# Layer-norm statistics of two token blocks in one VectorE instruction that reads them interleaved

## The chip, the cores and the metric

The kernel runs on one core of one Trainium2 chip. The metric is the device time of one execution in microseconds (us), lower is better. In what follows PE is TensorE (its matmuls; PEld its weight loads), DVE is VectorE, ACT is ScalarE, POOL is GpSimd and SP is SyncE.

## What is computed

The input x has 4096 tokens of 256 channels. It is layer-normalised; the normalised rows xn feed two branches whose results are added to x: a Hyena-like block (normalise again, project to 768 columns, two causal convolutions of 128 taps over time with gates between, an output projection) and a gated feed-forward network with integer weights.

```python
def _layernorm(x, axis=-1, eps=1e-05):
    m = jnp.mean(x, axis=axis, keepdims=True)
    v = jnp.var(x, axis=axis, keepdims=True)
    return (x - m) / jnp.sqrt(v + eps)
...
        xn = _layernorm(x, gamma, beta)
        proj = (xn @ W_in + b_in).reshape(Bn, Tn, ORDER + 1, Dn)
        v = proj[:, :, 0, :]
        y = jnp.transpose(v, (0, 2, 1))
        for i, kern in enumerate((k0, k1)):
            xi = jnp.transpose(proj[:, :, i + 1, :], (0, 2, 1))
            y = _fft_conv(y, kern, Tn) * xi
        y = jnp.transpose(y, (0, 2, 1))
        y = y @ W_out + b_out
        return residual + y
...
        gate = jnp.einsum('bsd,hd->bsh', x, wg)
        up = jnp.einsum('bsd,hd->bsh', x, wu)
        h = jax.nn.silu(gate) * up
        return jnp.einsum('bsh,dh->bsd', h, wd)
...
    x = L0_attn_x
    xn = _layernorm(x, axis=-1)
    x = x + _L0_attn_ref(xn, ...) + _L0_ffn_ref(xn, ...)
```

What the change touches is only the mean m and the variance v of each of the 4096 rows of x.

## The kernel before

The 4096 tokens are 32 blocks of 128. A block has its tokens on the 128 partitions, and block b is `res[:, b, :]`, 256 f32 side by side in SBUF; block b + 1 lies 1024 bytes further on. SP loads x in five batches (blocks 0 to 3, 4 to 7, 8 to 15, 16 to 23, 24 to 31; the borders are `CUTS`).

The program has a first stage (to about 70 us), a main stage of 16 groups G (convolutions, with the feed-forward steps beside them) and a last stage that projects out. The change lies in the first stage. There every engine runs through steps b = 1, 2, ... 43, written out by hand, and semaphores tie the engines together:

- DVE, step b: subtracts the rounded half of block b - 1 (`split_x`, L887, tile xT), may normalise a block two ahead (L879, tile ybuf), aggregates the statistics taken one step earlier (`aggregate`, L872, tile mv), may reverse a block (L901, tile xr), evicts projections (L895, L908), takes new statistics (`block_stats`, L866, tile stats), and does its share of the weight preparation (L946 the low half of the projection weights, L1047 the maxima of the taps, L940 the maxima of the integer weights).
- POOL, for each batch: `first_scales` (L1255 to L1258, tile lns: mean and variance become a factor and an offset) once `stats_ready` has counted that batch; `second_scales` (L1264 to L1267); its own normalised blocks (L1272); the weight load issues (L1331 to L1334); and L1327, the other low half of the projection weights.
- ACT normalises (L681), rounds (L685) and reverses (L692) blocks.
- PE, step b: transposes block b once it is normalised (L345), projects blocks that are a few steps back (L320, banks bank_p and bank_c), and transposes integer weights (L394).

The statistics instruction (`bn_stats`, in the profile BATCH_NORM_STATS2) takes 256 elements of a row and gives six numbers: count, mean and sum of squared deviations of the elements at even places, and the same of those at odd places. The aggregation (`bn_aggr`, in the profile BATCH_NORM_AGGREGATE) makes one mean and one variance out of the six. How many blocks get their statistics in which step is the table `STATS`; blocks 0 to 7 get theirs before step 1, ahead of `column_scales` (L924 to L932), which makes the projection weights. The `stats` tile has room for eight blocks and is used in turn.

```python
    STATS = {1: 4, 2: 1, 3: 1, 4: 2, 5: 2, 6: 1, 7: 2, 8: 4, 9: 1, 11: 1, 12: 1, 13: 1, 16: 3}
...
                    ins = nc.vector.bn_stats(stats[:, b % 8, :], res[:, b, :])
...
                    ins = nc.vector.bn_aggr(mv[:, b, :], stats[:, b % 8, :])
```

Of the kernel before, what the change touches and what calls it, by code (L numbers as in the profile page):

```python
# [6 lines left out]
P = 128  # L7
ALU = mybir.AluOpType
# [9 lines left out]
def hyena_ffn_kernel(nc, x, W_in, b_in, k0, k1, gamma, beta, W_out, b_out, w_gate, w_up, w_down, out):  # L18
# [8 lines left out]
    T, D = x.shape[1], x.shape[2]  # L27
    K = k0.shape[2]
    H = w_gate.shape[0]
    NB = T // P  # L30
# [7 lines left out]
    CUTS = (0, 4, 8, 16, 24, NB)  # L38
# [7 lines left out]

    STATS = {1: 4, 2: 1, 3: 1, 4: 2, 5: 2, 6: 1, 7: 2, 8: 4, 9: 1, 11: 1, 12: 1, 13: 1, 16: 3}
    WHI, WLO, PLO, SDG, KMAX = 3, 4, 5, 4, 5
# [36 lines left out]
    EPS = 1e-5  # L85
# [14 lines left out]
    with ExitStack() as ctx:  # L100
        def sb(name, shape, dt=F32):
            return ctx.enter_context(nc.sbuf_tensor(name, shape, dt))

        def sem(name):
            return ctx.enter_context(nc.semaphore(name))
# [5 lines left out]
        res = sb("res", [P, NB, D])  # L111
# [15 lines left out]
        ident32 = sb("ident32", [P, P])  # L127
        stats = sb("stats", [P, 8, 6])
        mv = sb("mv", [P, NB, 2])
        lns = sb("lns", [P, 8, NB])  # L130
# [14 lines left out]
        r1, r2, r1p, nmr, ls0, r2r = (lns[:, i, :] for i in range(6))  # L145
# [8 lines left out]
        def borrow(name, flat, n):  # L154
# [40 lines left out]
        x_loaded = [sem(f"x_loaded{i}") for i in range(NBATCH)]  # L195
# [10 lines left out]
        sdg_mm, sdg_ready = sem("sdg_mm"), sem("sdg_ready")  # L206
        half_stats, stats_ready, r_ready, r2_ready, r2r_ready = (
            sem("half_stats"), sem("stats_ready"), sem("r_ready"), sem("r2_ready"), sem("r2r_ready"))
        xn_ready, x_tp, xh_ready, xl_ready, xra_ready, xrv_ready = (
# [50 lines left out]
        def batch_of(b):  # L260
            return max(m for m in range(NBATCH) if CUTS[m] <= b)
# [584 lines left out]
        def _(dve):  # L846
# [14 lines left out]

            def block_stats(first, last):
                for b in range(first, last):
                    if b in CUTS:
                        dve.wait_ge(x_loaded[batch_of(b)], 16)
                    ins = nc.vector.bn_stats(stats[:, b % 8, :], res[:, b, :])  # L866
                ins.then_inc(half_stats, 1)

            def aggregate(first, last, batches):
                dve.wait_ge(half_stats, batches)  # L870
                for b in range(first, last):
                    ins = nc.vector.bn_aggr(mv[:, b, :], stats[:, b % 8, :])  # L872
                    if b + 1 in CUTS:
                        ins.then_inc(stats_ready, 1)

# [105 lines left out]
            def prepare(slot):  # L981
# [15 lines left out]
                for q in range(PAIRS):  # L997
                    if PAIR_V[q] == slot:
# [8 lines left out]
                                           op0=ALU.mult, op1=ALU.add).then_inc(gnorm_ready, 1)  # L1007
            block_stats(0, 4)
            aggregate(0, 4, 1)
            block_stats(4, 8)  # L1010
            aggregate(4, 8, 2)
            column_scales()

            done = [8]
            for b in range(1, LAST):
                if b - 1 < NB:
                    split_x(b - 1)
                if b + 2 < NB and NORM[b + 2] == "V":
                    normalise(b + 2)
                if b - 1 in STATS and 1 < b <= max(STATS):  # L1020
                    n = STATS[b - 1]
                    aggregate(done[0] - n, done[0], 2 + sum(1 for t in STATS if t < b))
                for p in range(NB):
# [5 lines left out]
                for n in range(NPB):  # L1029
                    if V_AT[PB * n + PB - 1] + 1 == b:  # L1030
                        scale_bank(n)
                if b in STATS:
                    block_stats(done[0], done[0] + STATS[b])
                    done[0] += STATS[b]
                if b == max(STATS):

                    aggregate(NB - STATS[b], NB, 2 + len(STATS))
                if b == WLO:
# [87 lines left out]
            for G in range(NG):  # L1126
                n = SG * G - LATE
# [101 lines left out]
        def _(pool):  # L1229
            chain = [0]  # L1230

            def link(ins):

                chain[0] += 1
                ins.then_inc(pool_chain, 1)
                pool.wait_ge(pool_chain, chain[0])
# [13 lines left out]
            def first_scales(m):  # L1250
                pool.wait_ge(stats_ready, m + 1)
                s = slice(CUTS[m], CUTS[m + 1])
                mean, var = mv[:, s, 0], mv[:, s, 1]
                half_power = minus_half[:, 0:s.stop - s.start]
                link(nc.gpsimd.tensor_scalar(ls0[:, s], var, EPS, None, ALU.add))  # L1255
                link(nc.gpsimd.tensor_tensor(r1[:, s], ls0[:, s], half_power, ALU.pow))
                link(nc.gpsimd.tensor_tensor(nmr[:, s], mean, r1[:, s], ALU.mult))
                nc.gpsimd.tensor_scalar(nmr[:, s], nmr[:, s], -1.0, None, ALU.mult).then_inc(r_ready, 1)  # L1258

            def second_scales(m):  # L1260
                s = slice(CUTS[m], CUTS[m + 1])
                var = mv[:, s, 1]
                half_power = minus_half[:, 0:s.stop - s.start]
                link(nc.gpsimd.tensor_tensor(ls0[:, s], var, r1[:, s], ALU.mult))  # L1264
                link(nc.gpsimd.tensor_tensor(ls0[:, s], ls0[:, s], r1[:, s], ALU.mult))
                link(nc.gpsimd.tensor_scalar(ls0[:, s], ls0[:, s], EPS, None, ALU.add))
                nc.gpsimd.tensor_tensor(r2[:, s], ls0[:, s], half_power, ALU.pow).then_inc(r2_ready, 1)  # L1267
# [154 lines left out]
```

## Time and profile before

| | |
|---|---|
| median of 3 runs | 333.57 us (333.04 to 333.96) |
| profiled execution, its own time | 333.88 us |
| profiled execution, span of the core | 332.0 us |
| granted TensorE clock, mean | 0.997 of full speed |
| PE busy | 303.2 us, 91% of the span |
| DVE busy | 264.5 us, 80% |
| POOL busy | 212.5 us, 64% |
| ACT busy | 179.3 us, 54% |
| first stage | about 0 to 70 us |

Busy time is added up per engine. On DVE the records of neighbouring instructions overlap by some 0.08 us: the next one starts while the last is still in the pipeline. What an instruction costs its engine is therefore the time from its start to the start of the next one, called its slot below, and not its duration. In rows of the timeline the columns are the start, the time, the engine, the line, the operation, what is written and read, and how many instructions were merged into the row; a bracket tells how long the engine had been idle before it and what ended that.

### The profile page before, as it was taken

To read this page: it belongs to the slowest core of one execution; us is meant where nothing else is said; L and a number is where in the kernel's file an instruction comes from. 1 tells how busy PE (TensorE), PEld (TensorE's weight loads), DVE (VectorE), ACT (ScalarE), POOL (GpSimd) and SP (SyncE) were. 2 spreads that over 40 slices of the span, in tenths; PEclk is the share of its full clock that TensorE was granted. 3 is DMA by queue.
4 is the path that set the end of the run, shared out by engine and by line. 5 is a ranking of instruction groups with operands and counts; after the bars stand their busy time and mean duration, and the time that the engine had idled before them with its cause. 6 is when DMAs were issued, how large, how long until landed. Compare 5 with 4: busy or idle time off the path is not lost.

```text
span 332.0 us, 11912 instructions
## 1 busy us (share of the span) xinstructions
PE 303.2 (91%) x4945; PEld 237.7 (72%) x4945; DVE 264.5 (80%) x534; ACT 179.3 (54%) x385; POOL 212.5 (64%) x290
## 2 busy tenths in 40 slices
PE   0379989999999999999999999999999999989993
PEld 0168777887778768777787777778777866658982
DVE  2798999976976888595887879779687777879994
ACT  3676588654544344443545444444445353479991
POOL 3699979377887877788777768868878563200000
PEclk9999999999999999999999999999999999999998
DMA  7994006827987869677786867879688788001345
GB/s 233 350 350 81 2 9 218 347 71 305 387 297 259 337 241 388 201 328 287 282 360 232 360 239 297 323 258 377 218 333 304 279 360 324 8 1 66 126 155 167
DMA packets 22033, 81.01 MB, mean 244 GB/s; under 512 B 1494, under 2 KB 13402, under 8 KB 13786
## 3 DMA queue, kind: packets, MB, share of 16 engines
q1 hardware_dynamic: 19458, 77.47, 62.6%
q0 software_dynamic: 2368, 2.36, 3.7%
q8 instruction: 41, 0.67, 0.8%
q10 hardware_dynamic: 152, 0.40, 0.4%
q14 instruction: 14, 0.11, 0.1%
HBM read 75.50 MB, written 4.72 MB: 242 GB/s over the span
## 4 chain that ended last, share of the span: by engine, by line
PE 49%; DVE 20%; POOL 11%; ACT 8%; issue 7%; DMA 3%; SPq 0%; POOLq 0%; DVEq 0%
PE bank_c L320 13%; PE bank_p L320 11%; PE bank_g L320 9%; PE bank_u L320 9%; PE bank_d L320 7%; ACT vx L834 3%; ACT vx L826 3%; DVE sgh L1055 3%; DMA res<-in_L_attn_x 3%; DVE hhl L1060 2%; DVE vx L908 2%; POOL ybuf L1374 2%; DVE xT L887 2%; POOL vhl L1288 2%; DVE stats L866 1%
## 5 line engine op out<-in xcount | busy, mean ns | idle before, releaser
L320 PE MATMUL bank_d<-wd,hhl 128*128 128x256 f16 x384 | 84.3, 271 | 0.3 <-DVE hhl L1060 0.2
L320 PEld LDWEIGHTS bank_p<-wq,xT 128*128 128x128 f16 x1536 | 70.1, 98 | 19.1 <-issue 4.3
L320 PE MATMUL bank_p<-wq,xT 128*128 128x64 f16 x1536 | 79.6, 193 | 2.5 <-POOL wq L1327 2.4
L320 PE MATMUL bank_u<-xT,wgu 128*128 128x512 f16 x192 | 66.2, 378 | 0.4 <-DVE sgh L1055 0.4
L320 PE MATMUL bank_g<-xT,wgu 128*128 128x512 f16 x192 | 66.2, 377 | 0.5 <-ACT sgh L750 0.5
L320 PEld LDWEIGHTS bank_c<-ybuf,bands 128*128 128x128 f16 x1024 | 51.8, 96 | 16.6
L320 PEld LDWEIGHTS bank_c<-vhl,bands 128*128 128x128 f16 x1024 | 49.0, 96 | 19.6 <-issue 4.4
L320 PE MATMUL bank_c<-ybuf,bands 128*128 128x64 f16 (+3 forms) x1024 | 60.3, 184 | 0.0
L320 PE MATMUL bank_c<-vhl,bands 128*128 128x64 f16 (+3 forms) x1024 | 57.3, 184 | 2.9 <-POOL vhl L1288 1.2
L756 ACT CAST hhl<-sgh 128x512 f16<-128x512 f32 x48 | 29.7, 619 | 49.4 <-DVE sgh L1055 49.4
L1060 DVE TENSOR_TENSOR hhl<-sgh,hhl 128x512 f16<-128x512 f32 x48 | 42.1, 878 | 13.3 <-ACT hhl L756 12.1
L1282 POOL TENSOR_TENSOR vx<-vx,bias 128x512 f32<-128x512 f32 x32 | 36.6, 1146 | 23.0 <-DVE vx L908 23.0
L1380 POOL TENSOR_TENSOR x1y<-ybuf,vx 128x256 f32<-128x256 f32 x32 | 23.2, 727 | 30.0 <-DVE ybuf L1076 30.0
L764 ACT COPY xr<-bank_c 128x256 f32<-128x256 f32 x64 | 23.7, 370 | 31.9 <-PE bank_c L320 31.6
L750 ACT ACTIVATE sgh<-bank_g,cst 128x512 f32<-128x512 f32 x48 | 32.8, 682 | 14.9 <-PE bank_g L320 14.7
L1076 DVE TENSOR_TENSOR ybuf<-bank_c,xr 128x256 f32<-128x256 f32 x64 | 26.6, 418 | 15.6 <-ACT xr L764 15.4
L320 PEld LDWEIGHTS bank_d<-wd,hhl 128*128 128x128 f16 x384 | 36.9, 97 | 2.8 <-issue 1.1
L1055 DVE SCALAR_TENSOR_TENSOR sgh<-bank_u,cst,sgh 128x512 f32<-128x512 f32 x48 | 35.5, 739 | 0.0
L1081 DVE SCALAR_TENSOR_TENSOR ybuf<-ybuf 128x256 f16<-128x256 f32 x32 | 26.1, 827 | 5.4 <-ACT ybuf L771 5.4
L1288 POOL TENSOR_TENSOR vhl<-vx,vhl 128x256 f16<-128x256 f32 x32 | 24.5, 768 | 7.3 <-ACT vhl L705 7.2
L320 PE MATMUL bank_c<-wq,xr 128*128 128x256 f16 x192 | 26.8, 279 | 0.7 <-DVE xr L901 0.6
L1374 POOL TENSOR_TENSOR ybuf<-ybuf,x1y 128x256 f32<-128x256 f32 x32 | 26.2, 841 | 1.6 <-DVE ybuf L1076 1.6
(189 smaller groups left out, 553.3 us busy)
## 6 DMA issues: line engine op xcount, KB each, us to landing
bands<-taps_seq SPq DMA_DIRECT2D x64, 1024.0 KB, 8.1
out<-res SPq DMA_DIRECT2D x8, 512.0 KB, 2.9
res<-in_L_attn_x SPq DMA_DIRECT2D x3, 1024.0 KB, 11.0
res<-in_L_attn_x SPq DMA_DIRECT2D x2, 512.0 KB, 6.2
bands<-in_L_attn_W_in SPq DMA_DIRECT2D x1, 768.0 KB, 6.0
wgu<-in_L_ffn_w_gate POOLq DMA_DIRECT2D x1, 768.0 KB, 8.3
wgu<-in_L_ffn_w_up POOLq DMA_DIRECT2D x1, 768.0 KB, 9.4
wd<-in_L_ffn_w_down POOLq DMA_DIRECT2D x2, 384.0 KB, 9.8
```

The costliest lines, as they stand in the source:

```text
L320: return nc.tensor.matmul(o, w, m, start=start, stop=stop, skip_group_check=True)
L750: nc.scalar.activation(sgh[:, n % 2, :], bank_g[:, :], ACT.Silu, scale=c(C_GS)).then_inc(sg_ready, 1)
L756: nc.scalar.copy(hhl[:, n % 3, 0, :], sgh[:, n % 2, :]).then_inc(hh_ready, 1)
L764: nc.scalar.copy(conv_lo[:, h, :, :], o[:, 1, :, :]).then_inc(lo_copied, 1)
L1055: nc.vector.scalar_tensor_tensor(out=sgh[:, n % 2, :], in0=bank_u[:, :], scalar=c(C_HS), in1=sgh[:, n % 2, :], op0=ALU.mult, op1=ALU.mult) ...
L1060: nc.vector.tensor_tensor(hhl[:, n % 3, 1, :], sgh[:, n % 2, :], hhl[:, n % 3, 0, :], ALU.subtract).then_inc(hl_ready, 1)
L1076: nc.vector.tensor_tensor(y1f[:, h * CH:(h + 1) * CH, :], o[:, 0, :, :], conv_lo[:, h, :, :], ALU.add).then_inc(c_added, 1)
L1081: nc.vector.scalar_tensor_tensor(out=y1hl[:, 1, chans, :], in0=y1f[:, chans, :], scalar=Y1_SCALE, in1=y1hl[:, 0, chans, :], op0=ALU.mult, ...
L1282: nc.gpsimd.tensor_tensor(tile, tile, off, ALU.add).then_inc(vx_ready, 1)
L1288: nc.gpsimd.tensor_tensor(vhl[:, r % 2, 1, :, blocks], vx[:, r % 2, 0, :, blocks], vhl[:, r % 2, 0, :, blocks], ALU.subtract).then_inc(vl_ ...
L1374: nc.gpsimd.tensor_tensor(y1f[:, chans, :], y1f[:, chans, :], x1y2[:, G * CG + h * CH:G * CG + (h + 1) * CH, :], ALU.mult).then_inc(y1_rea ...
L1380: nc.gpsimd.tensor_tensor(x1y2[:, G * CG + h * CH:G * CG + (h + 1) * CH, :], y1f[:, h * CH:(h + 1) * CH, :], vx[:, r % 2, 1, g * CG + h * ...
```

## The change

One statistics instruction now takes two neighbouring blocks. Its input is the pair of blocks in the order channel 0 of the first, channel 0 of the second, channel 1 of the first, and so on, 512 elements: the elements at even places are one block, those at odd places the other. So the six numbers that come out are count, mean and sum of squares of each block, and the aggregation is dropped. The `mv` tile becomes a view of `stats`, which now has room for all pairs (three numbers a block); POOL takes the sum of squares times 1/256 in place of the variance, as a second operation inside instructions that it had already. The wait on `half_stats` and the semaphore are gone. The table `STATS` counts pairs now, and it places them otherwise: 4 pairs before step 1 as before, 12 pairs in the steps 1 to 16.

```diff
-    STATS = {1: 4, 2: 1, 3: 1, 4: 2, 5: 2, 6: 1, 7: 2, 8: 4, 9: 1, 11: 1, 12: 1, 13: 1, 16: 3}
+    STATS = {1: 2, 2: 1, 4: 1, 5: 1, 6: 1, 7: 2, 9: 1, 11: 1, 13: 1, 16: 1}
...
-        stats = sb("stats", [P, 8, 6])
-        mv = sb("mv", [P, NB, 2])
+        stats = sb("stats", [P, NB // 2, 6])
+        mv = stats[:, :, :].rearrange("p j s -> p (j s)").rearrange("p (b s) -> p b s", s=3)
...
-            def block_stats(first, last):
-                for b in range(first, last):
-                    if b in CUTS:
-                        dve.wait_ge(x_loaded[batch_of(b)], 16)
-                    ins = nc.vector.bn_stats(stats[:, b % 8, :], res[:, b, :])
-                ins.then_inc(half_stats, 1)
-
-            def aggregate(first, last, batches):
-                dve.wait_ge(half_stats, batches)
-                for b in range(first, last):
-                    ins = nc.vector.bn_aggr(mv[:, b, :], stats[:, b % 8, :])
-                    if b + 1 in CUTS:
-                        ins.then_inc(stats_ready, 1)
+            def pair_stats(j):
+                b = 2 * j
+                if b in CUTS:
+                    dve.wait_ge(x_loaded[batch_of(b)], 16)
+                ins = nc.vector.bn_stats(stats[:, j, :], res[:, b:b + 2, :].rearrange("p b d -> p d b"))
+                if b + 2 in CUTS:
+                    ins.then_inc(stats_ready, 1)
...
-                mean, var = mv[:, s, 0], mv[:, s, 1]
+                mean, m2 = mv[:, s, 1], mv[:, s, 2]
...
-                link(nc.gpsimd.tensor_scalar(ls0[:, s], var, EPS, None, ALU.add))
+                link(nc.gpsimd.tensor_scalar(ls0[:, s], m2, 1.0 / D, EPS, ALU.mult, ALU.add))
```

On DVE, the steps 1 to 4 of the first stage. xT is the rounded block of a step (its low half is written there), res the loaded x, bands the raw projection weights and wq their halves. Before:

```order
L887 TENSOR_TENSOR xT<-bank_g,xT 128x2x128
L866 BN_STATS stats<-res 128x6 x4
L887 TENSOR_TENSOR xT<-bank_u,xT 128x2x128
L872 BN_AGGR mv<-stats 128x2 x4
L866 BN_STATS stats<-res 128x6
L887 TENSOR_TENSOR xT<-bank_d,xT 128x2x128
L872 BN_AGGR mv<-stats 128x2
L866 BN_STATS stats<-res 128x6
L887 TENSOR_TENSOR xT<-bank_g,xT 128x2x128
L872 BN_AGGR mv<-stats 128x2
L866 BN_STATS stats<-res 128x6 x2
L946 TENSOR_TENSOR wq<-bands,wq 128x768
```

The same place in the changed kernel (its L881 is L887 of before, its L940 is L946 of before):

```order
L881 TENSOR_TENSOR xT<-bank_g,xT 128x2x128
L866 BN_STATS stats<-res 128x6 x2
L881 TENSOR_TENSOR xT<-bank_u,xT 128x2x128
L866 BN_STATS stats<-res 128x6
L881 TENSOR_TENSOR xT<-bank_d,xT 128x2x128
L881 TENSOR_TENSOR xT<-bank_g,xT 128x2x128
L866 BN_STATS stats<-res 128x6
L940 TENSOR_TENSOR wq<-bands,wq 128x768
```

Eight statistics and six aggregations stood between the first xT and the weights; now four pair statistics, so again eight blocks, stand there.

On DVE, the steps 8 and 9, before (x1y is an evicted projection, pmw the maxima of the integer weights):

```order
L887 TENSOR_TENSOR xT<-bank_u,xT 128x2x128
L872 BN_AGGR mv<-stats 128x2 x2
L901 COPY xr<-xT 128x4x128
L895 TENSOR_TENSOR x1y<-bank_c,lns 128x256x2
L866 BN_STATS stats<-res 128x6 x4
L940 TENSOR_REDUCE pmw<-wgu 128x1
L887 TENSOR_TENSOR xT<-bank_d,xT 128x2x128
L872 BN_AGGR mv<-stats 128x2 x4
L866 BN_STATS stats<-res 128x6
L886 COPY lns<-bank_g 128x4
```

And in the changed kernel:

```order
L881 TENSOR_TENSOR xT<-bank_u,xT 128x2x128
L895 COPY xr<-xT 128x4x128
L889 TENSOR_TENSOR x1y<-bank_c,lns 128x256x2
L934 TENSOR_REDUCE pmw<-wgu 128x1
L881 TENSOR_TENSOR xT<-bank_d,xT 128x2x128
L866 BN_STATS stats<-res 128x6
L880 COPY lns<-bank_g 128x4
```

Step 8 has no statistics any more: the four that stood there are partly done by step 7 and partly later. PE, ACT and SP have the same instructions in the same order, and POOL the same instructions with other operands.

## Rows read from the trace of the kernel before

**Rows 1.** The page's first part: busy us, share of the span, instructions.

```profile
PE 303.2 (91%) x4945; PEld 237.7 (72%) x4945; DVE 264.5 (80%) x534; ACT 179.3 (54%) x385; POOL 212.5 (64%) x290
```

**Rows 2.** Busy time by window: window and its length, then us busy per engine.

```profile
25.00:40.00 15.00, 15.00 (x166) 12.43 (x166) 13.52 (x44) 8.72 (x20) 13.52 (x29) 1.00 0.22 44
40.00:62.00 22.00, 19.64 (x229) 16.50 (x225) 21.25 (x67) 18.66 (x42) 17.42 (x26) 1.00 0.43 157
62.00:70.00 8.00, 7.34 (x86) 6.62 (x86) 7.56 (x16) 4.05 (x9) 2.44 (x4) 1.00 0.40 166
```

**Rows 3.** The chain of waits, 8 to 50 us: start us, us, what.

```profile
10.22 1.42 DVE stats L866 x4
12.12 0.24 POOL lns L1255
...
43.48 1.00 DVE stats L866 x3
```

**Rows 4.** The timeline of DVE, 10 to 45 us.

```profile
10.22 1.41 DVE L866 BATCH_NORM_STATS2 stats<-res 128x6 f32<-128x256 f32 x4 [2.47 <-DMA res<-in_L_attn_x]
11.66 0.38 DVE L872 BATCH_NORM_AGGREGATE mv<-stats 128x2 f32<-128x6 f32 x4
11.96 0.99 DVE L924 SCALAR_TENSOR_TENSOR bands<-bank_c,bands 128x384 f32<-128x384 f32 x2
...
25.91 0.16 DVE L886 COPY lns<-bank_g 128x4 f32<-128x4 f32 x1 [1.16 <-ACT xT L685]
...
28.28 0.42 DVE L887 TENSOR_TENSOR xT<-bank_u,xT 128x256 f16<-128x256 f32 x1 [0.56 <-ACT xT L685]
...
37.85 2.45 DVE L940 TENSOR_REDUCE pmw<-wgu 128x1 f32<-128x512 f32 x4
...
40.61 0.41 DVE L879 TENSOR_SCALAR ybuf<-res,lns 128x256 f32<-128x256 f32 x1
...
41.92 0.31 DVE L901 COPY xr<-xT 128x512 f16<-128x512 f16 x1
...
43.40 1.07 DVE L866 BATCH_NORM_STATS2 stats<-res 128x6 f32<-128x256 f32 x3
44.50 0.32 DVE L872 BATCH_NORM_AGGREGATE mv<-stats 128x2 f32<-128x6 f32 x3
44.73 0.39 DVE L887 TENSOR_TENSOR xT<-bank_u,xT 128x256 f16<-128x256 f32 x1
```

**Rows 5.** The timeline of PE: its first projection, and its waits for DVE to 50 us.

```profile
22.96 0.48 PE L320 MATMUL bank_p<-wq,xT 128*128 128x64 f16 x6 [2.39 <-POOL wq L1327]
...
41.08 0.44 PE L345 MATMUL bank_u<-ident,ybuf 128*128 128x128 f32 x2 [0.26 <-DVE ybuf L879]
...
42.29 0.83 PE L320 MATMUL bank_c<-wq,xr 128*128 128x256 f16 x6 [0.60 <-DVE xr L901]
...
46.44 0.33 PE L445 MATMUL bank_d<-ident,pmw 128*128 128x128 f32 x1 [0.23 <-DVE pmw L940]
```

**Rows 6.** The timeline of POOL, the last batch's scales.

```profile
44.90 0.25 POOL L1255 TENSOR_SCALAR lns<-mv 128x8 f32<-128x8 f32 x1 [2.15 <-DVE mv L872]
```

**Rows 7.** One line's instructions each: count, duration ns min/median/max, first and last start us, shapes.

```profile
L866 DVE BATCH_NORM_STATS2 stats<-res x32: 392/410/427, 5.9 to 44.1; 128x6 f32<-128x256 f32 x32
...
L940 DVE TENSOR_REDUCE pmw<-wgu x6: 670/676/681, 27.0 to 39.6; 128x1 f32<-128x512 f32 x6
...
L1086 DVE TENSOR_REDUCE ymax<-x1y x16: 1041/1052/1058, 82.4 to 290.4; 128x32 f32<-128x512 f32 x16
...
L1178 DVE TENSOR_REDUCE stats<-ymax x1: 967/967/967, 287.6 to 287.6; 128x32 f32<-128x480 f32 x1
...
L895 DVE TENSOR_TENSOR x1y<-bank_c,lns x10: 681/689/693, 29.0 to 68.3; 128x512 f32<-128x512 f32 x10
...
L826 ACT ACTIVATE vx<-x1y,lns x32: 731/782/896, 294.3 to 322.8; 128x256 f32<-128x256 f32 x32
...
L771 ACT ACTIVATE ybuf<-ybuf x32: 416/417/419, 73.6 to 282.5; 128x256 f16<-128x256 f32 x32
```

More of the change, by code:

```diff
@@ L206, in hyena_ffn_kernel @@
         sdg_mm, sdg_ready = sem("sdg_mm"), sem("sdg_ready")
-        half_stats, stats_ready, r_ready, r2_ready, r2r_ready = (
-            sem("half_stats"), sem("stats_ready"), sem("r_ready"), sem("r2_ready"), sem("r2r_ready"))
+        stats_ready, r_ready, r2_ready, r2r_ready = (
+            sem("stats_ready"), sem("r_ready"), sem("r2_ready"), sem("r2r_ready"))
         xn_ready, x_tp, xh_ready, xl_ready, xra_ready, xrv_ready = (
@@ L1007, in _ @@
                                            op0=ALU.mult, op1=ALU.add).then_inc(gnorm_ready, 1)
[L1008 to L1011, printed above, removed]
+            for j in range(4):
+                pair_stats(j)
             column_scales()
-            done = [8]
+            done = [4]
             for b in range(1, LAST):
@@ L1019, in _ @@
                     normalise(b + 2)
-                if b - 1 in STATS and 1 < b <= max(STATS):
-                    n = STATS[b - 1]
-                    aggregate(done[0] - n, done[0], 2 + sum(1 for t in STATS if t < b))
                 for p in range(NB):
@@ L1031, in _ @@
                         scale_bank(n)
[L1032 to L1037, printed above, removed]
+                for _ in range(STATS.get(b, 0)):
+                    pair_stats(done[0])
+                    done[0] += 1
                 if b == WLO:
@@ L1261, in second_scales @@
                 s = slice(CUTS[m], CUTS[m + 1])
-                var = mv[:, s, 1]
+                m2 = mv[:, s, 2]
                 half_power = minus_half[:, 0:s.stop - s.start]
-                link(nc.gpsimd.tensor_tensor(ls0[:, s], var, r1[:, s], ALU.mult))
+                link(nc.gpsimd.tensor_tensor(ls0[:, s], m2, r1[:, s], ALU.mult))
                 link(nc.gpsimd.tensor_tensor(ls0[:, s], ls0[:, s], r1[:, s], ALU.mult))
-                link(nc.gpsimd.tensor_scalar(ls0[:, s], ls0[:, s], EPS, None, ALU.add))
+                link(nc.gpsimd.tensor_scalar(ls0[:, s], ls0[:, s], 1.0 / D, EPS, ALU.mult, ALU.add))
                 nc.gpsimd.tensor_tensor(r2[:, s], ls0[:, s], half_power, ALU.pow).then_inc(r2_ready, 1)
```

## The prediction

> **What bounds the kernel now.** I read the busy shares first: PE is busy for 91% of the span and DVE for 80% [rows 1], so on the average PE is the bound. But the change lies in the first stage, so the next view is the busy time by window. From 25 to 40 us PE is busy for all 15.00 us. From 40 to 62 us it is 19.64 of 22, while DVE is busy for 21.25 of 22 [rows 2]. So there DVE is the fuller engine, and PE's idle time, 2.4 us, is what a quicker DVE could give back. From 62 us on PE is at 7.34 of 8 and takes over again.
>
> The chain of waits says the same, and it holds two places where statistics stand on the path themselves [rows 3]. The first is at 10.22 us: DVE has waited 2.47 us for the second batch of x [rows 4], takes the statistics of blocks 4 to 7, and behind them go POOL's scales (12.12), POOL's issues, POOL's half of the weights (L1327) and PE's first projection at 22.96, which waited 2.39 us for that half [rows 5]. The second is at 43.48, three statistics in a row in the stretch that DVE bounds. PE's own waits show where DVE's lateness reaches it: 0.26 us at 41.08 for a block that DVE normalises, 0.60 at 42.29 for a reversed block, 0.23 at 46.44 for the maxima [rows 5]. Between 12 and 41 us only idle time of DVE tells how far it can fall behind: it waits 1.16 us before 25.91 and 0.56 us before 28.28, both times for ACT, which waits for PE [rows 4]. That is a reserve of 1.72 us. From 28.28 on it has none.
>
> **What is removed.** A statistics instruction takes 410 ns [rows 7], but its slot is shorter: from 10.22 to 11.66 four of them and a little, (1.41 - 0.41) / 3 = 0.33 us each [rows 4]. Four aggregations take from 11.66 to 11.96, the last three of the chain from 44.50 to 44.73 [rows 4]: 0.08 us each. From 10.22 to 44.73 there are 28 of each kind (blocks 4 to 31), so 28 x 0.33 + 28 x 0.08 = 9.3 + 2.3 = 11.6 us of DVE go. Blocks 0 to 3 come before the DMA wait at 10.22 and cost nothing: the 2.47 us of that wait cover them, four slots of about 1 us at most against 1.6 now; what they delay is POOL's first scales by 0.2 us, and behind these PE has its norms to do anyway.
>
> **What is added.** 14 pair statistics from 10.22 on, each with one slot c. The trace has no such instruction, so c is bounded from both sides.
>
> - From below: 512 f32 elements that lie side by side. Four reductions of that size take 2.45 us in a row, (2.45 - 0.68) / 3 = 0.59 us each [rows 4], and one takes 676 ns [rows 7]. The 410 ns of a statistics over 256 elements and these 676 over 512 lie 266 ns apart, 1.04 ns an element, so the two operations run at one rate, and c = 0.60.
> - From above: the elements do not lie side by side. Each read is 1024 bytes from the one before it. The nearest rows are the reductions at L1086 and L1178, which read SBUF tiles (channels by 32 blocks, groups by 32 blocks) across their rows, in steps of 128 bytes. L1086 has 512 elements like L940, and takes 1052 ns where L940 takes 676; L1178 takes 967 for 480 [rows 7]. That they give 32 results and not one could be the reason instead of the step, and the rows here cannot part the two. ACT shows a like pair, though: 256 elements at steps of 128 bytes in 782 ns (L826), side by side in 417 (L771) [rows 7], and there the number of results is the same. With the 376 ns more of the reductions, c = 0.60 + 0.376 = 0.98. If every read costs two of the 1.04 ns, it is 0.60 + 0.53 = 1.13; if it costs what ACT pays, (782 - 417) / 256 = 1.43 ns more an element, 0.60 + 0.73 = 1.33.
>
> Against a penalty speaks L895, 512 elements taken from two halves of a bank in turn, 1024 bytes apart, in 689 ns [rows 7], which is no more than L940 takes for contiguous ones. But it reads PSUM, and the changed instruction reads SBUF, like L1086, L1178 and L826. So I take c = 0.98.
>
> The Trainium skill has a rule for this (Advanced Engine Details and Errata, SBUF Cachelines): lines of 16 bytes, at least two hits on a line to hide the latency of the SRAM, and a penalty where each access goes to another line. By that rule every read of the interleaved pair pays, since its neighbour lies in another line; the page gives no size. The rows above agree with it for steps of 128 bytes; that it holds for two lines that are read in turn, four times each, no run here shows.
>
> **Where it lands.** DVE's lateness against before is a running sum over the steps, with c = 0.98, and idle time that DVE had is taken off where it lies.
>
> - Ahead of step 1: 2 x 0.98 against 4 x 0.33 + 4 x 0.08 with the gaps, 11.96 - 10.22 = 1.74. That is +0.21 us, for DVE's weights and for POOL's scales alike. It goes straight to PE's first projection: 22.96 becomes 23.17, and the saturated stretch of PE begins that much later.
> - Steps 1 to 7, ten blocks' worth of work more tightly packed: before 13 statistics and 11 aggregations, 13 x 0.33 + 11 x 0.08 = 5.1 us, now 8 pairs, 7.8 us. That is +2.7, together +2.9, less the reserve of 1.72: DVE is 1.2 us late at step 8. The steps' slack covers that: PE transposes block b when block b - 3 is split, which leaves it more than one step, and a step of PE is 1.2 to 1.7 us long. DVE's half of the weights (L946, step 4) comes 1.1 us later; the wait at 22.96 ends with POOL's half [rows 5], and I take it that DVE's stays the earlier of the two.
> - Step 8: four statistics and two aggregations are gone, -1.5 us. DVE is now 0.2 us ahead.
> - Steps 9 to 13: before 4 statistics and 8 aggregations, 1.9 us; now 3 pairs, 2.9 us. At 40.61, the block that PE waits for at 41.08, DVE is 0.8 us late, and 0.7 at 41.92 (one aggregation less), the reversed block of the wait at 42.29. PE is then some 0.7 us behind.
> - Step 16: 0.98 against three statistics and three aggregations, 44.73 - 43.40 = 1.33 [rows 4]. DVE is 0.35 us late at 44.73, PE 0.7 less the 0.23 us that it idled before 46.44, so 0.47.
>
> Behind that nothing differs up to the end: DVE is the bound to 62 us, then PE, and a shift is passed on whole. POOL, which waited 2.15 us for the last batch [rows 6], gets it 0.35 us later, and has no more to do than before. What POOL's instructions do more (one factor, on 4 or 8 elements) has no price that the rows could show, and I take nothing. So +0.5 us. The sum is made against the profiled execution's 333.88 us, which is 0.3 over the median of the runs shown; on the median, 333.57 + 0.5 = 334.1 us.
>
> **The rivals.**
>
> - *The interleaved read is free*, c = 0.60, as L895's row would have it. Ahead of step 1 it is 1.20 - 1.74 = -0.54 us, on POOL's chain and PE's start at once. DVE drops 1.5 us in step 8 and then meets ACT and PE, which are only 0.54 us ahead: it waits, and at 40.61 is 1.2 us ahead, so PE loses its idle 0.26, then 0.53 of its 0.60, then its 0.23 at 46.44: 0.54 + 0.26 + 0.53 + 0.23 = 1.6 us ahead, and DVE's stretch to 62 us starts that much earlier. 332.0 us. This is the case on the other side. It decides from c = 0.95 downward: 14 x 0.95 is 11.6 + 1.72, where the running sum ends at nothing.
> - *The read costs two cycles an element or more*, c = 1.13 to 1.33. From c = 0.95 upward each tenth of a microsecond costs 14 x 0.1 = 1.4 us, since the reserve is used up: +2.5 us at 1.13 (336.1), +5.3 us at 1.33 (338.9). For it speaks that the pair's two rows are 1024 bytes apart, further than any row here, and ACT's price; against it, that the DVE rows stop at 376 ns for 512.
> - *PE hides it.* The new work sits where PE is full (25 to 40 us), so DVE's lateness stays in its slack and only the 0.2 us at the start is left: 333.8. The table's retiming favours this, the waits at 41.08 and 42.29 speak against it. It is in the forecast's own range.
>
> **How the numbers follow.** A measurement of this kernel can tell about 0.3%, 1.0 us, from no change. The forecast, c near 0.98 with or without PE's cover, 0.50; free 0.28; two cycles or more 0.19; something else 0.03. Within the forecast the slope of 14 makes a little a lot: c = 1.02 is already +1.0 us. So of its 0.50 I give 0.10 to slower and 0.02 to faster. Faster 0.32, same 0.39, slower 0.29. The forecast's own range is 333.5 to 335.2; the whole one reaches down to the free case with its spread, 331.7, and up to c = 1.13, 336.2.
>
> **What would show it right or wrong.** In the changed profile: the mean duration of the statistics line, 1.06 us by the forecast (slots of 0.98), 0.68 if the read is free, over 1.2 in the second rival. DVE's idle time before the split at steps 7 and 8 gone, and no statistics in step 8. PE's first projection at 23.2 (22.4 if free), its wait at 41 us longer than 0.26 (gone if free). POOL's wait for the last batch still over 2 us. The prediction is wrong if the duration is 1.06 and the time still falls by over 1 us, for then DVE's slots in the first stage do not set the end; or if a queue that I left out, such as the load of batch 3 or 4 of x, ends a wait of the statistics.

## The result, and the profile after

Six runs of the changed kernel have a median of 331.61 us (330.56 to 333.67), against 333.96 us (333.04 to 334.68) for six runs of the kernel before on the same chip: ratio 0.9929, 95% interval 0.9905 to 0.9954, so 0.7% faster. On a second chip the ratio was 0.9886 (0.9851 to 0.9920); the kernel before was slower there (335.73 us), the changed one nearly the same (331.93 us). The forecast was 334.1 us and no change that can be told; the result is just below its range. One execution of the kernel before and one of early_pairs, below, took 438.0 and 437.4 us at a lower granted clock and are in no figure here.

The first thing to look at is the statistics line, on which the whole sum rested. The instructions of that line of the changed kernel (duration ns min/median/max, as in [rows 7]):

```profile
L866 DVE BATCH_NORM_STATS2 stats<-res x16: 681/693/703, 5.8 to 42.8; 128x6 f32<-128x512 f32 x16
```

693 ns, not 1.06 us: the lower bound of the prediction, to the hundredth. The timeline of DVE in the changed kernel gives the slots and the idle time; L881 is L887 of before, L895 is L901, L889 is L895:

```profile
10.09 1.31 DVE L866 BATCH_NORM_STATS2 stats<-res 128x6 f32<-128x512 f32 x2 [3.04 <-DMA res<-in_L_attn_x]
11.31 1.01 DVE L918 SCALAR_TENSOR_TENSOR bands<-bank_c,bands 128x384 f32<-128x384 f32 x2
...
19.15 0.95 DVE L940 TENSOR_TENSOR wq<-bands,wq 128x768 f16<-128x768 f32 x1
...
24.69 0.16 DVE L880 COPY lns<-bank_g 128x4 f32<-128x4 f32 x1 [0.92 <-ACT xT L685]
...
27.59 0.42 DVE L881 TENSOR_TENSOR xT<-bank_u,xT 128x256 f16<-128x256 f32 x1 [0.61 <-ACT xT L685]
...
34.50 0.69 DVE L889 TENSOR_TENSOR x1y<-bank_c,lns 128x512 f32<-128x512 f32 x1 [0.47 <-PE bank_c L320]
...
37.04 2.44 DVE L934 TENSOR_REDUCE pmw<-wgu 128x1 f32<-128x512 f32 x4
...
41.05 0.60 DVE L895 COPY xr<-xT 128x512 f16<-128x512 f16 x1
...
42.82 0.69 DVE L866 BATCH_NORM_STATS2 stats<-res 128x6 f32<-128x512 f32 x1
43.44 0.40 DVE L881 TENSOR_TENSOR xT<-bank_u,xT 128x256 f16<-128x256 f32 x1
```

Two pairs take from 10.09 to 11.31, so the slot is 0.61 us, and the start takes 1.22 us where it took 1.74 [rows 4]. The split that stood at 44.73 stands at 43.44. DVE still has its idle time in front of 24.69 and 27.59, and a third piece of 0.47 us at 34.50; up to the split at 43.44 two more are 0.21 us and less. GpSimd's timeline has a row that the prediction did not expect to differ, its half of the weights (L1313, L1327 before). The changed kernel first, then the kernel before, with DVE's half (L946):

```profile
19.91 1.69 POOL L1313 TENSOR_TENSOR wq<-bands,wq 128x768 f16<-128x768 f32 x1
...
20.38 0.94 DVE L946 TENSOR_TENSOR wq<-bands,wq 128x768 f16<-128x768 f32 x1
20.59 2.23 POOL L1327 TENSOR_TENSOR wq<-bands,wq 128x768 f16<-128x768 f32 x1
```

Before, GpSimd's half started while DVE's was running and took 2.23 us. The timeline of PE in the changed kernel, its first projection, its waits for DVE to 62 us, and the first convolution:

```profile
21.74 0.48 PE L320 MATMUL bank_p<-wq,xT 128*128 128x64 f16 x6 [1.81 <-POOL wq L1313]
...
41.71 0.83 PE L320 MATMUL bank_c<-wq,xr 128*128 128x256 f16 x6 [0.83 <-DVE xr L895]
...
59.97 0.41 PE L345 MATMUL bank_g<-ident,ybuf 128*128 128x128 f32 x2 [0.58 <-DVE xT L881]
...
67.97 1.88 PE L320 MATMUL bank_c<-vhl,bands 128*128 128x64 f16 x64 [0.65 <-issue]
```

The first projection is 1.22 us earlier than in [rows 5]. Of the waits of [rows 5] those at 41.08 and 46.44 are gone, and the one for the reversed block has grown from 0.60 to 0.83. In what follows I use the start of the first convolution, the last row, as the mark of where the first stage ends: 67.97 us here, and in the kernel before

```profile
70.18 1.88 PE L320 MATMUL bank_c<-vhl,bands 128*128 128x64 f16 x64 [0.65 <-issue]
```

The 2.2 us between them are nearly all of the 2.4 us between the two profiled executions (331.48 and 333.88 us). The rest of the program, 263.5 us against 263.7, did not take part in this pair.

### The profile page after: what moved, and what is told of

Its sections match the earlier page's. It is cut to its first block, busy times and chain, and to the rows that moved or that the text cites. A ratio compares the mean times of both kernels' runs of the same rounds, so it can differ in the third digit from the quotient of the medians.

```text
span 329.6 us, 11864 instructions
## 1 busy us (share of the span) xinstructions
PE 302.8 (92%) x4945; PEld 238.2 (72%) x4945; DVE 261.1 (79%) x486; ACT 178.8 (54%) x385; POOL 210.4 (64%) x290
## 4 chain that ended last, share of the span: by engine, by line
PE 53%; DVE 17%; POOL 10%; ACT 8%; issue 6%; DMA 3%; SPq 0%; POOLq 0%; DVEq 0%
PE bank_c L320 15%; PE bank_p L320 11%; PE bank_g L320 9%; PE bank_u L320 9%; PE bank_d L320 8%; ACT vx L834 3%; ACT vx L826 3%; DVE sgh L1041 3%; DMA res<-in_L_attn_x 3%; DVE hhl L1046 2%; DVE vx L902 2%; POOL ybuf L1360 2%; POOL vhl L1274 2%; ACT hhl L756 1%; POOL res L1308 1%
## 5 line engine op out<-in xcount | busy, mean ns | idle before, releaser
L1046 DVE TENSOR_TENSOR hhl<-sgh,hhl 128x512 f16<-128x512 f32 x48 | 43.8, 912 | 13.3 <-ACT hhl L756 12.1
L1067 DVE SCALAR_TENSOR_TENSOR ybuf<-ybuf 128x256 f16<-128x256 f32 x32 | 24.4, 775 | 5.3 <-ACT ybuf L771 5.3
L1360 POOL TENSOR_TENSOR ybuf<-ybuf,x1y 128x256 f32<-128x256 f32 x32 | 26.2, 841 | 1.6 <-DVE ybuf L1062 1.6
```

Of the source, the lines that this page charges most:

```text
L1046: nc.vector.tensor_tensor(hhl[:, n % 3, 1, :], sgh[:, n % 2, :], hhl[:, n % 3, 0, :], ALU.subtract).then_inc(hl_ready, 1)
L1067: nc.vector.scalar_tensor_tensor(out=y1hl[:, 1, chans, :], in0=y1f[:, chans, :], scalar=Y1_SCALE, in1=y1hl[:, 0, chans, :], op0=ALU.mult, ...
L1360: nc.gpsimd.tensor_tensor(y1f[:, chans, :], y1f[:, chans, :], x1y2[:, G * CG + h * CH:G * CG + (h + 1) * CH, :], ALU.mult).then_inc(y1_rea ...
```

## The experiments

Ratios are to the kernel before on the same chip, with 95% intervals; the kernel before itself ran from 332.6 to 337.5 us over these chips, so intervals are about 0.3% to each side. The mark is that of each run's one profile. From the mark to the end the profiled executions take 263.3 to 264.1 us, and 264.9 to 265.5 in the four kernels that shared one chip (early_pairs, late_pairs, padded, weights_first), so the mark follows the first stage more closely than the time does. It has a spread of its own. The last column is the time of twelve matmuls of PE near 25 us, which differs even between two profiles of one kernel (last section); where it is short, all that follows in the first stage can be earlier by the difference.

| run | ratio | first projection | first convolution | twelve matmuls |
|---|---|---|---|---|
| before, two profiles | 1 | 22.96, 22.86 | 70.18, 70.00 | 1.70, 2.27 |
| changed, two profiles | 0.9929, 0.9886 | 21.74, 21.71 | 67.97, 68.04 | 2.23, 2.31 |
| contig_pair | 0.990 (0.9864 to 0.9937) | 21.64 | 67.01 | 1.71 |
| old_places | 0.9951 (0.9922 to 0.9981) | 21.82 | 67.98 | 1.76 |
| new_places | 0.9967 (0.9936 to 0.9998) | 22.75 | 69.31 | 2.25 |
| early_pairs | 0.9946 (0.9918 to 0.9975) | 22.44 | 69.48 | 2.31 |
| late_pairs | 0.9942 (0.9911 to 0.9974) | 22.26 | 68.50 | 2.23 |
| weights_first | 0.9982 (0.9954 to 1.0010) | 22.29 | 69.34 | 2.25 |
| padded | 1.0005 (0.9974 to 1.0036) | 23.02 | 70.62 | 2.75 |
| maxima_spread | 0.9853 (0.9818 to 0.9888) | 21.75 | 66.19 | 1.85 |

**The price of a read by itself (reads).** Nine reads, four times each, behind the changed kernel's last instruction.

```diff
+            side = x1y2[:, 0:CG, :].rearrange("p c b -> p (c b)")
+            rows32 = side.rearrange("p (b c) -> p b c", c=CG)
+            cols32 = x1y2[:, 0:CG, :].rearrange("p c b -> p b c")
+            cols2 = x1y2[:, :, 0:2].rearrange("p c b -> p b c")
+            pair = res[:, 0:2, :].rearrange("p b d -> p d b")
```

> The changed kernel, with 36 VectorE instructions added behind its last one, four of each of nine kinds; only their durations and slots are read, not the time. Reductions of 512 f32 from SBUF: side by side to 1 result; side by side to 32 results of 16; in steps of 128 bytes to 32 results (the form of L1086); in steps of 128 bytes to 2 results of 256; two rows 1024 bytes apart in turn to 1 result. Statistics of 512: side by side; two rows in turn; steps of 128 bytes in runs of 256; steps of 128 bytes in runs of 16. Theory A, any step reads at one element a cycle and the 376 ns of L1086 are the price of its 32 results: side by side to 32 results takes 1.05 us, steps of 128 bytes to 2 results 0.68, all four statistics 0.69. Theory B, steps of 128 bytes cost and two rows in turn do not, because each line is read again at the next turn: 32 results side by side 0.68, both reductions in steps of 128 bytes about 1.05, statistics in such steps about 1.06 and in turn 0.69.

The groups of those lines (busy us and mean ns of one behind the first bar). In order of line: L1224 side by side to 1 result, L1226 side by side to 32, L1228 steps of 128 bytes to 32, L1230 steps of 128 bytes to 2, L1232 two rows in turn to 1, then statistics, L1234 side by side, L1236 two rows in turn, L1238 and L1240 steps of 128 bytes:

```profile
L1240 DVE BATCH_NORM_STATS2 wout<-x1y 128x6 f32<-128x512 f32 x4 | 3.8, 1008 | 0.0
L1238 DVE BATCH_NORM_STATS2 wout<-x1y 128x6 f32<-128x512 f32 x4 | 3.7, 1006 | 0.0
L1228 DVE TENSOR_REDUCE wout<-x1y 128x32 f32<-128x512 f32 x4 | 3.7, 997 | 0.0
L1230 DVE TENSOR_REDUCE wout<-x1y 128x2 f32<-128x512 f32 x4 | 3.7, 996 | 0.0
L1236 DVE BATCH_NORM_STATS2 wout<-res 128x6 f32<-128x512 f32 x4 | 2.5, 692 | 0.0
L1232 DVE TENSOR_REDUCE wout<-res 128x1 f32<-128x512 f32 x4 | 2.5, 685 | 0.0
L1234 DVE BATCH_NORM_STATS2 wout<-x1y 128x6 f32<-128x512 f32 x4 | 2.5, 684 | 0.0
L1226 DVE TENSOR_REDUCE wout<-x1y 128x32 f32<-128x512 f32 x4 | 2.5, 675 | 0.0
L1224 DVE TENSOR_REDUCE wout<-x1y 128x1 f32<-128x512 f32 x4 | 2.5, 674 | 0.0
```

Theory B holds and A falls. The number of results costs nothing (675 against 674 ns). Steps of 128 bytes do cost, 0.32 us on 512 elements, in a reduction and in statistics alike, so [rows 7] had been read rightly. But two rows in turn, 1024 bytes apart, cost 8 to 11 ns. The nearest row was near in kind and had the wrong answer.

**How far that goes (turns).** Eight more reads, all as statistics of 512.

```diff
+            step8 = whole[:, 0:1024].rearrange("p (n s) -> p n s", s=2)[:, :, 0]
...
+            turn2_once = whole[:, 0:2048].rearrange("p (h n s) -> p n h s", h=2, s=4)[:, :, :, 0]
+            turn4 = res[:, 0:4, 0:128].rearrange("p b d -> p d b")
```

> The changed kernel with 32 VectorE statistics instructions of 512 f32 added behind its last one, four of each of eight reads; only durations and slots are read. Steps of 8, 16 and 32 bytes; two rows 4096 bytes apart in turn with steps of 16 bytes within each, so that no 16 bytes are read twice; 4, 8, 16 and 32 rows 1024 bytes apart in turn, side by side within a row. Known so far: side by side and two rows in turn have slots of 0.60 us, steps of 128 bytes 0.90. Theory B, what costs is a 16-byte piece that is used once, and pieces used before are kept for some reads: step 8 free (0.60), steps 16 and 32 cost (0.90), two rows in turn with steps of 16 bytes cost (0.90), and of the rows in turn all up to some number are free. Theory C, what counts is where successive reads fall and not what was read before: reads 1024 or 4096 bytes apart are free whatever lies in them, so two rows with steps of 16 bytes and 4 to 32 rows in turn all have 0.60, while steps of 16 and 32 bytes may cost or not.

In order of line: L1231 steps of 8 bytes, L1233 of 16, L1235 of 32, L1237 two rows in turn with steps of 16 bytes in each, then L1239, L1241, L1243 and L1245 with 4, 8, 16 and 32 rows in turn:

```profile
L1237 DVE BATCH_NORM_STATS2 wout<-res 128x6 f32<-128x512 f32 x4 | 4.2, 1100 | 0.0
L1235 DVE BATCH_NORM_STATS2 wout<-res 128x6 f32<-128x512 f32 x4 | 4.0, 1055 | 0.0
L1233 DVE BATCH_NORM_STATS2 wout<-res 128x6 f32<-128x512 f32 x4 | 3.9, 1036 | 0.0
L1239 DVE BATCH_NORM_STATS2 wout<-res 128x6 f32<-128x512 f32 x4 | 3.8, 1007 | 0.0
L1241 DVE BATCH_NORM_STATS2 wout<-res 128x6 f32<-128x512 f32 x4 | 3.8, 1000 | 0.0
L1243 DVE BATCH_NORM_STATS2 wout<-res 128x6 f32<-128x512 f32 x4 | 3.7, 998 | 0.0
L1245 DVE BATCH_NORM_STATS2 wout<-res 128x6 f32<-128x512 f32 x4 | 3.7, 996 | 0.0
L1231 DVE BATCH_NORM_STATS2 wout<-res 128x6 f32<-128x512 f32 x4 | 2.5, 680 | 0.0
```

Theory C falls: two rows in turn cost the full surcharge (1100 ns) once each 16-byte piece is used for one read only. (These two rows lie 4096 bytes apart, those of the pair 1024; no run changed the distance alone.) Theory B holds with a short memory: two rows are free, four are not (1007 ns), and three were not tried. The Trainium skill (Advanced Engine Details and Errata, SBUF Cachelines) asks for at least two hits on a line of 16 bytes. By that rule steps of 8 bytes are free and steps of 16 and more are not; both measurements agree. It also says that accesses to a different line pay; for two rows in turn, whose every read goes to another line than the one before, the measurement (692 ns) decides against that reading of it.

**The same in the kernel (contig_pair).**

```diff
-                ins = nc.vector.bn_stats(stats[:, j, :], res[:, b:b + 2, :].rearrange("p b d -> p d b"))
+                ins = nc.vector.bn_stats(stats[:, j, :], res[:, b:b + 2, :].rearrange("p b d -> p (b d)"))
```

> The changed kernel with one thing changed: the pair statistics read their two blocks side by side, so that the even and odd places mix the two blocks and the statistics are no longer those of the layer norm; everything else is done as before. If the interleaved read costs nothing at all: statistics 0.69 us long as in the changed kernel, ratio to the kernel before 0.993, as the change has. If it costs a little that the duration hides (a longer slot, or a port kept from GpSimd): the slot falls below the 0.60 us seen and the ratio to 0.990 or less.

A pair takes 681 ns as the median against 693, and its slot is 0.60 us. The ratio, 0.990, is the one of the second case, but its interval holds the first case too, and it overlaps that of the change. The mark is 1.0 us earlier, and the rows say where that comes from. 0.10 us is there at the first projection. 0.52 is the row of the twelve matmuls (1.71 us for 2.23). 0.32 is the reversed block near 41 us, whose copy took 0.28 us for 0.60: in the changed kernel it starts at 41.05, behind a subtraction of GpSimd; here it starts just ahead of it, and it is GpSimd's that is longer. The timeline rows, the changed kernel's subtraction first, then contig_pair's copy and subtraction:

```profile
40.84 0.67 POOL L1294 TENSOR_TENSOR sgh<-bands,sgh 128x256 f16<-128x256 f32 x1
...
40.42 0.28 DVE L895 COPY xr<-xT 128x512 f16<-128x512 f16 x1
40.48 0.76 POOL L1294 TENSOR_TENSOR sgh<-bands,sgh 128x256 f16<-128x256 f32 x1
```

The three make 0.94 us, and PE's projection of that block starts 0.95 us earlier (40.76 for 41.71). What the interleaved read can have cost by its durations is 14 times 11 ns, 0.15 us.

**The slot put back (padded).**

```diff
+                nc.vector.bn_stats(spare[:, j, :], res[:, b, :])
                 ins = nc.vector.bn_stats(stats[:, j, :], res[:, b:b + 2, :].rearrange("p b d -> p d b"))
```

> The changed kernel with one more statistics instruction of 256 elements in front of each pair, its result unused: the pair's slot becomes 0.61 + 0.33 = 0.94 us, nearly the 0.98 on which the prediction's sum was made. If that sum was right but for the slot: 14 x 0.94 less the 11.6 us and the reserve of 1.7 is about nothing, VectorE at the split of step 17 as in the kernel before within 0.3 us, ratio 0.999 to 1.001. If other steps of the sum failed too (GpSimd's and VectorE's overlap elsewhere), the ratio is 0.996 or less, or over 1.002.

With the slot at 0.94 us the gain is gone: 1.0005, mark 70.62. That the prediction's sum gives no change for the slot it assumed is confirmed for the time, to the 0.3% that can be told. DVE's reserve is used up, as the sum has it: of its idle time one piece of 0.19 us is left up to 48 us, at 33.70. The split of step 17 is at 46.03 us, later than in the two profiles of the kernel before (44.73 and 45.34) by 1.3 and 0.7 us, and outside the 0.3 us expected. The rows put that on PE and not on the slots: the twelve matmuls took 2.75 us here, and the projection behind them starts at 28.95 us for 27.68 and 28.14, later by 1.3 and 0.8. DVE's half of the weights took twice its time and became the one that PE waited for, but this alone moved the first projection by no more than 0.2 us (23.02 for 22.96 and 22.86). The timeline rows of this kernel, DVE, POOL and PE:

```profile
21.04 1.89 DVE L942 TENSOR_TENSOR wq<-bands,wq 128x768 f16<-128x768 f32 x1
...
20.48 1.63 POOL L1315 TENSOR_TENSOR wq<-bands,wq 128x768 f16<-128x768 f32 x1
...
23.02 0.48 PE L321 MATMUL bank_p<-wq,xT 128*128 128x64 f16 x6 [2.37 <-DVE wq L942]
...
25.98 2.75 PE L321 MATMUL bank_c<-wq,xr 128*128 128x256 f16 x12
```

**The two halves of the weights (weights_first).** The kernel before, with one swap on DVE in step 4.

```diff
+                if b == WLO:
+                    split_input_weights()
                 if b in STATS:
                     block_stats(done[0], done[0] + STATS[b])
                     done[0] += STATS[b]
...
-                if b == WLO:
-                    split_input_weights()
```

> The kernel before with one swap on VectorE in step 4: its half of the weights (L946) goes ahead of the two statistics and not behind them, so it starts at 19.7 and ends before GpSimd's half starts at 20.6. Theory that GpSimd's half was 2.23 us and not 1.69 because VectorE's ran beside it (0.7 us of overlap): it now takes 1.7 us, the first projection comes 0.5 us earlier, ratio 0.9985 to 1.000 depending on whether VectorE's waits at 41 us swallow it. Rival, that the length is from something else (the statistics beside it, the clock of the day): still 2.2 us.

DVE's half now starts at 19.66 us, and in the timeline of POOL its half is short:

```profile
20.52 1.63 POOL L1327 TENSOR_TENSOR wq<-bands,wq 128x768 f16<-128x768 f32 x1
```

1.63 us for 2.23, and the first projection at 22.29. So the half is longer when DVE's runs beside it, and whichever of the two starts second pays: GpSimd's in both profiles of the kernel before, in new_places and in early_pairs (2.22 to 2.28 us), DVE's in padded (1.89). The mark is 0.7 to 0.8 us earlier; the ratio, 0.9982, does not tell itself from 1. The Trainium skill has this rule (SBUF — State Buffer, Who interferes with whom): a VectorE instruction with two inputs from SBUF contends with a GpSimd instruction that reads SBUF. These rows agree, at 0.6 to 0.95 us for tiles of 128 by 768.

**The start alone, the rest alone (early_pairs, late_pairs).** Pairs for blocks 0 to 7 only, or for 8 to 31 only; the others keep their statistics and aggregation.

```diff
-            for j in range(4):
-                pair_stats(j)
+            block_stats(0, 4)
+            aggregate(0, 4, 1)
+            block_stats(4, 8)
+            aggregate(4, 8, 2)
```

> Only the first eight blocks (ahead of step 1) get pair statistics without aggregation; blocks 8 to 31 are done as in the kernel before, in its places. Theory that the start gives its 0.5 us straight through GpSimd's chain, and GpSimd's half of the weights (L1327) is another 0.5 us shorter because VectorE's half no longer runs beside it: first projection 0.5 to 1.1 us earlier, but VectorE, as loaded as before, keeps the waits at 41 to 46 us, so the end gains 0.5 to 1.0 us; ratio 0.997 to 0.9985. Theory that the shorter sum later on carries nearly all: 1.000.

> Only blocks 8 to 31 get pair statistics without aggregation, in the places of the change; the first eight are done as in the kernel before. Theory of parts that add up: the change's -0.7% less what the early pairs alone give, 0.995 to 0.9965. Theory that PE's start limits all (PE is full from 25 to 40 us, so VectorE can run ahead of it by no more than PE's own idle 1.1 us): not below 0.9965, and VectorE shows more idle time between 28 and 40 us than the 1.7 us it had in front of 28.3.

Marks of 69.48 and 68.50. Against the profile of the kernel before whose twelve matmuls are alike (70.00) they are 0.5 and 1.5 us earlier, together the 2.0 of the whole change by the same comparison. The kernel before has no profile on the chip of these two. The two ratios are too near to 0.994 and too wide to divide the gain; that of early_pairs is below what either theory expected, while its mark fits the first. In early_pairs GpSimd's half is still 2.28 us long, in late_pairs it is 1.70: the overlap is removed by the new order of step 4 (four pairs' slots, 2.4 us, ahead of DVE's half where eight blocks and six aggregations took 3.1), not by the earlier start.

**Instruction or table (old_places, new_places).**

```diff
-    STATS = {1: 2, 2: 1, 4: 1, 5: 1, 6: 1, 7: 2, 9: 1, 11: 1, 13: 1, 16: 1}
+    STATS = {1: 2, 3: 1, 4: 1, 5: 1, 7: 1, 8: 2, 9: 1, 12: 1, 16: 2}
```

> The changed kernel with the pairs placed as nearly as pairs allow where the blocks stood before (steps 1: 2, 3: 1, 4: 1, 5: 1, 7: 1, 8: 2, 9: 1, 12: 1, 16: 2). Theory that the time comes from the start and from VectorE's shorter sum: the places matter little, statistics ready 0.5 us earlier at the start as in the change, and VectorE at the split of step 17 about 0.3 us later than in the change; ratio 0.993 to 0.995. Theory that the places carry the gain (no statistics in step 8, one pair fewer after it): the ratio goes back to 0.998 or more.

> The kernel before with its own statistics and aggregations, placed block by block as in the change (steps 1: 4, 2: 2, 4: 2, 5: 2, 6: 2, 7: 4, 9: 2, 11: 2, 13: 2, 16: 2); the start is as before. Theory that the start and the shorter sum carry the gain: three blocks (1.2 us) move in front of step 8 and fit into VectorE's 1.7 us of reserve, so VectorE is up to 1.2 us earlier at 41 us and TensorE loses its idle 0.26 and some of its 0.60 us there, 0.5 to 0.9 us in all; ratio 0.997 to 0.9985. Theory that the places carry it all: 0.993 to 0.994. Third: no change, 0.9995 to 1.0005, because the same idle time shows again at the next wait.

With pairs the old places have the mark of the new, 67.98 and 67.97, and the ratios' intervals overlap. But the profile of old_places has the short row of twelve matmuls (1.76 us for 2.23), and PE's wait of 0.23 us for the maxima is back, at 45.12 us. So a worth of the new places of up to 0.5 us is neither shown nor excluded; 0.998 or more, the case in which the places carry the gain, is excluded by the mark and at the edge of the interval by the time. With the old instructions the new places alone move the mark to 69.31, 0.7 to 0.9 us earlier, ratio 0.9967, and here the row of twelve matmuls (2.25) is that of the later profile of the kernel before. So the table has a worth where DVE is long; how much of it the shorter instruction leaves is open.

**The spread of one profile (before_again, after_again).** Both kernels unchanged.

> The kernel before, unchanged, profiled a second time: how far the places in time move from one execution to the next. In its first profile two small VectorE instructions behind the flag (L860, L962) took 0.51 and 0.50 us and L970 0.41, where all other kernels so far had 0.20, 0.27 and 0.16. If that is the kernel's own, from GpSimd's work beside it, it comes back, and so does a start of the convolutions at 70.2 us; if it is chance, the small ones are short and the convolutions start near 69.4. GpSimd's half of the weights (L1327) takes 2.2 us by either.

> The changed kernel, unchanged, profiled a second time and timed beside the kernel before on this chip. First projection again at 21.7 us and GpSimd's half of the weights 1.7 us long; the time at which TensorE's matmuls become short (near 26.2 us before) may differ and with it the start of the convolutions, 67.0 to 68.0 us. Ratio 0.991 to 0.995.

The small instructions behind the flag were short this time (0.20, 0.27 and 0.16 us), so their 0.8 us in the first profile was chance. The mark came back nevertheless, 70.00, since in this execution the twelve matmuls took 2.27 us and not 1.70. The timeline row of PE in before_again, and in after_again below it:

```profile
25.82 2.27 PE L320 MATMUL bank_c<-wq,xr 128*128 128x256 f16 x12
...
24.66 2.31 PE L320 MATMUL bank_c<-wq,xr 128*128 128x256 f16 x12
```

This pair is the one to compare: 2.0 us at the mark, 1.6 at the end (333.45 and 331.89 us); the first pair had 2.2 and 2.4. The ratio on this chip, 0.9886, is below the 0.991 expected, and the medians differ by 3.8 us, more than any mark explains. The profiled execution of the kernel before was shorter than all eleven timed ones beside it (334.33 to 337.47), so no trace shows what made those longer, and that stays open.

**A better version (maxima_spread).**

```diff
-    MAXIMA = (7, 8, 13, 13, 13, 13, 14, 15, 17)
+    MAXIMA = (7, 7, 8, 11, 13, 13, 14, 15, 17)
```

> The changed kernel with three of VectorE's maxima of the integer weights (0.60 us slots) moved into steps where it sat idle: the table of the steps is 7, 7, 8, 11, 13, 13, 14, 15, 17 in place of 7, 8, 13, 13, 13, 13, 14, 15, 17. VectorE was idle 0.61 us ahead of the split of step 8 and 0.47 us in step 12, and has four maxima in a row in step 13, behind which TensorE waits 0.83 us for a reversed block at 41.7. Theory that this wait is the last of TensorE's in the stretch that VectorE's order makes: 0.6 to 0.9 us earlier than the changed kernel at 46 us and at the start of the convolutions, ratio to the kernel before 0.990 to 0.992. Rival: the idle time was needed (an eviction or a reversal comes late for TensorE by the new place), or the wait only moves to the next block; then the ratio is that of the changed kernel.

Six runs, median 330.75 us, ratio 0.9853 (0.9818 to 0.9888), where the changed kernel had 0.9886 beside it; the medians differ by 1.2 us. The intervals of the two overlap; of the six executions five are below all six of the changed kernel on this chip. The mark is 66.19 us, 1.8 earlier than the changed kernel's where 0.6 to 0.9 was expected. 0.4 of that is the row of twelve matmuls (1.85 us). That leaves 1.4, of which PE's wait of 0.83 us is the part that the theory named; the rest was not followed up. The ratio, too, is below the 0.990 to 0.992 expected. The waits of PE from 30 to 62 us, as the view of waits has them (us in total, times, longest), are down to one line:

```profile
PE bank_g L345 <- DVE xT L881: 0.6, 1, 0.6
```

## Why the prediction was wrong

The step that failed is the price of the added instruction, "So I take c = 0.98". It measured 0.61 us. I took an upper bound from rows that read one element out of each 16-byte piece and put the interleaved pair beside them, because it reads SBUF as they do and its steps were longer still. The one row with the pair's own pattern, L895, I set aside because it reads PSUM; it had the right answer. What costs is not the length of a step but a piece that is used once, and in the pair each piece of 16 bytes is used four times, with one other piece in between. The prediction named this gap ("that it holds for two lines that are read in turn ... no run here shows") and then gave it 0.28, while the whole sum hung on it with a slope of 14 in the slot.

The sum itself held where its slot was put back, as far as 0.3% can tell: padded stayed at 1.0005. Its parts, one by one:

- **Removed.** Slots of 0.33 and 0.08 us and the reserve of 1.72 us were read rightly; but the reserve is not a constant of the kernel. In before_again, whose twelve matmuls are longer, DVE's two waits are 1.16 and 1.14 us, 2.30 together.
- **The start.** The free case had the first projection 0.54 us earlier; it came 1.15 to 1.22 earlier. About 0.5 is the shorter start (1.22 for 1.74), 0.54 the shorter half of the weights on GpSimd, which no part of the prediction priced, and 0.1 the earlier landing of x. This is the second failure: I costed L946 only by its lateness and not by what it does to the instruction beside it. weights_first shows it.
- **The free rival.** It gave 1.6 us and 332.0; measured were 2.0 to 2.2 at the mark and 331.6. That these lie so near is in part luck. In the pair of profiles with like matmuls the start gave 1.15 us for its 0.54, and the wait for the reversed block, from which it took 0.53, grew by 0.24. PE's projection of that block is 1.13 us earlier (42.90 to 41.77). What is passed on from there is DVE's gain, not PE's: 1.45 us at the reversal (42.55 to 41.10), 1.85 at the split of step 17 (45.34 to 43.49), where one pair stands in place of three statistics and three aggregations, and 2.0 at the mark.
- **Steps 7 to 13.** DVE's idle time in front of the splits of steps 7 and 8 stayed, as the free case wants. PE's waits at 41.08 and 46.44 went; that at 42.29 did not shrink but grew to 0.83, as PE came to it earlier and the reversal beside it took 0.60 us for 0.31 [rows 4].
- **Behind the first stage.** That a shift is passed on whole fits the first pair, 2.2 us at the mark and 2.4 at the end; in the second it is 2.0 and 1.6.
- **Two cycles or more, and PE hides it.** The pair measured 0.61 us, so the first did not come about. PE did not hide the slot either: at 0.94 us nothing was left of the gain that 0.61 brings.

## What to carry to other kernels

Where only far rows bound the cost of a new operation and the sum has a steep slope in it, price the mechanism and not the likeness: ask how often each 16-byte piece is used, and how many others are read between two uses. Statistics that return even and odd places apart take two rows at once if they are read in turn, and save the aggregation. When an instruction moves, look at what it then runs beside: of two subtractions over SBUF on VectorE and GpSimd the later one took up to twice its length here (1.89 us for 0.94), and a copy of VectorE behind a subtraction of GpSimd 0.60 us for 0.28.

## What the runs showed of the hardware

Reading SBUF at f32, VectorE needed 0.60 us of slot for 512 elements side by side, in steps of 8 bytes, or from two rows in turn, and 0.91 to 1.02 us in steps of 16, 32 or 128 bytes, from four or more rows in turn, and from two rows with steps of 16 bytes. Where between two and four rows the limit lies was not tried.

TensorE's matmuls became about half as long some time after 25 us, and not at one moment. In the changed kernel six of them (128 by 256) took 1.47 us at 22.03 us and 0.82 at 27.15, and the granted clock by window is 0.50, the lower of the two levels (1.2 GHz), from 16 to 26.2 us and 1.00 (2.4 GHz) from 26.3 on. PE had waited 3.57 us before 15.98, and it was busy without a gap from 22 us to the rise. The same twelve matmuls near 25 us took 1.70, 1.71, 1.76 or 1.85 us in some profiles, 2.23 to 2.31 in others and 2.75 in padded. PE is full there, so this moves what follows: in the two profiles of the kernel before, the projection behind them starts at 27.68 and 28.14 us, although the first projection was 0.1 us earlier in the second. That is as much as some of the effects studied here; differences of less than half a microsecond between single marks mean nothing unless this row is alike. In the other profiles the granted clock reads 1.00 throughout, with matmuls as long, so this column did not show it there; that it is the clock in these too is inferred from the like durations.
